# Four graph layers on one core: alternate quarters reversed in the first attention, padding columns left out in the second, an earlier operand load, a later transpose and a smaller closing product

## The chip, the cores and the metric

The kernel runs on one core of one Trainium2 chip. The metric is the device time of one execution in microseconds; the median of the runs is compared.

## The reference, cut to what matters

Four layers follow one another over 3125 nodes with 256 features and 100,000 edges, with a layer norm of the sum `x + layer(x)` behind each:

```
x = _layernorm(x + attention_4_heads(x))      # layer 0, q.k scores per edge, softmax over a node's edges
x = _layernorm(x + gat_4_heads(x))            # layer 1, leaky_relu(al_src[src] + al_dst[dst]), plus a 256-512-256 MLP
x = _layernorm(x + gin(gin(x)))               # layer 2, two plain neighbour sums with small MLPs
x = _layernorm(x + gat_1_head(gcn(x)))        # layer 3, a normalised sum, then attention with one head
...
e = jax.nn.leaky_relu(al_src[src] + al_dst[dst], NEG_SLOPE)
emax = jax.ops.segment_max(e, dst, num_segments=N)
ex = jnp.exp(e - emax[dst])
alpha = ex / denom[dst]
out = jax.ops.segment_sum(alpha[:, :, None] * h[src], dst, num_segments=N)
```

## The kernel before, in words

The graph is handled densely. Nodes are padded from N = 3125 to NPAD = 3200, 25 tiles of P = 128. Four stages run one behind the other, each a block with its own tiles and semaphores.

**Edge counts** (`build_counts`). For each tile of 128 targets the number of edges from every source is counted: VectorE writes one-hot rows (L431 to L435), TensorE multiplies them (`count`, L487) into four PSUM banks `p_g`, 400 columns each. A tile has two such counts (QPT = 2). Each ends with a closing product of zeros (L489) that adds nothing to the fourth bank and whose semaphore, `s_group`, releases ScalarE's `collect` (L552). ScalarE also writes the logarithms of the counts (L561). Between the counts TensorE does the projections of layer 0 (L174, L182) and turns count tiles for the logarithms (L497). Rows of counts, of their logarithms and of the queries, keys and values go to DRAM.

**First attention** (`attend` with `dot=True`, names `a_...`). A unit is one tile and one of 4 heads, so 100 units. A unit's 3200 weights lie in one of four buffers `sm`. TensorE's work is written out by hand in `body`, in four quarters u = 0 to 3 with TURNS = 8, 8, 8, 1 blocks of 128:

```
for u in range(ntu):
    if exists(at):
        turn(at, u)
    if dot and u in SCORE_AT and ahead(at, 2) is not None:
        score(ahead(at, 2), SCORE_AT[u])
    if behind(at, 1) is not None:
        weigh(behind(at, 1), u)
    if u == back_slot and behind(at, 2) is not None:
        turn_back(behind(at, 2))
    posts(pe, P_.pe, at, u)
```

- `turn` (L873) transposes the unit's own blocks into PSUM `p_t[u % 2]`; the trace calls its shape 128*128. It waits for the exp of its part and for the copy that frees the bank.
- `score` (L859) makes two of the eight pieces of q.k for the unit two ahead, on two halves of 64 rows at once (64*128), into `p_s[0]` and `p_s[1]`.
- `weigh` (L887) multiplies the previous unit's transposed weights by the values, 64 columns at a time (128*64). Its first quarter waits for `s_flip`, ScalarE's copy of the sums of the unit before.
- `turn_back` (L894, 128*128) turns the sums of the unit two behind. `posts` puts the output projection and norms of earlier tiles (L1267 to L1282, 128*128) into certain quarters; in this stage these are all quarters 1 and 3.

In the trace one `score` is 4 matmul records, 8 blocks of `weigh` are 16 records, and 8 of `turn` are 8. ScalarE goes through the quarters too: in each the copy of the transposed blocks back to `sm` (L930) and, in quarters 0 to 2, a part of the next unit's exp (L924); in front of them `flip` (L937), behind them `normalise` (L949). VectorE masks the two pieces of each `score` (L1010) and, during head 0 of a tile, prepares the next tile's mask from its logarithms in four parts (`mask_logs`, L997), right behind the masks of that quarter. SyncE issues the loads: `dot_tile` loads a tile's queries (L773) and its row of logarithms `full` (L777). For the first tile, the post's weights (`P_.load`) and the store of `full` come next, and only then the second tile's operands. ScalarE's queue loads the keys `kt` by head (L970) and the values (L972).

**Second attention** (`dot=False`). Two heads at a time, two passes over the 25 tiles, again 100 units. There are no scores: VectorE forms a unit's 3200 values with `lift` (L1026) and masks them and takes their maximum in `joined` (L1036); ScalarE takes the exp in three parts, EXPS = 0, 1024, 2048, 3200. TensorE's `turn`, `weigh` and `turn_back` are the same. In the second pass the posts hold the MLP with a Gelu (L1486, L1491, L1502).

**Sums and last attention** (`Tail`). Three dense neighbour sums (L1680, 25 tiles each), 25 blocks of two records a tile, with the small products of the tile before put behind certain blocks by `pe_post`. In the second sum VectorE's norm of the tile before (L1891, `x3`) is turned behind block s = 16 (L1699) and its projection follows behind s = 19. Then one attention head on full 128*128 shapes (L1757 turns, L1772 weighs).

## Time and profile before

| | us |
|---|---|
| median of 3 runs | 4048.44 |
| lowest, highest | 4046.75, 4051.8 |
| the profiled execution | 4048.74 |
| its span, first to last instruction | 4047.0 |

| engine | busy us in the span | share |
|---|---|---|
| TensorE (PE) | 3779.3 | 93% |
| TensorE weight load (PEld) | 2883.8 | 71% |
| VectorE (DVE) | 2334.7 | 58% |
| ScalarE (ACT) | 2057.9 | 51% |
| GpSimd (POOL) | 460.0 | 11% |

The span covers what lies between the first and the last instruction; 1.7 us lie around it. TensorE's busy time counts a matmul until its modelled end, so two neighbours overlap; the distance between two starts is the better measure of what an instruction costs in a stream.

### The profile page before, as it was taken

The page shows a single profiled execution, that of the slowest core. Times are in us where ns is not written, and L with a number is a line of the kernel's source. Part 1 is how long each engine was busy: PE and PEld are TensorE (multiplying, and loading weights), DVE is VectorE, ACT ScalarE, POOL GpSimd, SP SyncE. Part 2 cuts the span into 40 slices and gives each one's busy share as a digit, 9 for nine tenths or more (in the row PEclk, how much of TensorE's full clock was granted, in tenths as well). Part 3 has the DMA queues.
Part 4 walks back from the last instruction along what each step waited for, and adds up shares of the span by engine and source line. Part 5 has one row for each costly group of instructions (what it writes and reads, how often), then busy time and mean ns, then how long its engine had stood idle before and what let it go on. Part 6 is the DMA issues. An engine that isn't in the chain of part 4 may idle for free. (4 is left out here: it accounts for less than half of the span.)

```text
span 4047.0 us, 69966 instructions
## 1 busy us (share of the span) xinstructions
PE 3779.3 (93%) x27513; PEld 2883.8 (71%) x27514; DVE 2334.7 (58%) x4672; ACT 2057.9 (51%) x3697; POOL 460.0 (11%) x594
## 2 busy tenths in 40 slices
PE   4999969999999999679998988979999999999999
PEld 2656536666666666457777777768888888888888
DVE  7999935555555565289999899810012221004665
ACT  1555536666666666479998788810001000003554
POOL 0000000111111111100003455410000000000000
PEclk9999979999999999889999999989999999999999
DMA  1555572233233323153342232243333333333342
GB/s 53 234 202 234 205 239 98 90 107 107 87 105 96 103 90 108 46 200 115 115 177 100 87 108 94 92 154 141 141 141 132 132 134 136 130 130 135 137 147 69
DMA packets 177168, 521.22 MB, mean 129 GB/s; under 512 B 54304, under 2 KB 141680, under 8 KB 143728
## 3 DMA queue, kind: packets, MB, share of 16 engines
q1 hardware_dynamic: 176096, 510.62, 35.7%
q10 hardware_dynamic: 784, 6.55, 0.6%
q8 instruction: 205, 3.36, 0.3%
q14 instruction: 83, 0.68, 0.1%
HBM read 354.82 MB, written 162.29 MB: 128 GB/s over the span
## 5 line engine op out<-in xcount | busy, mean ns | idle before, releaser
L1680 PE MATMUL t_acc<-t_r,t_ct 128*128 128x256 f32 (+1 forms) x3750 | 855.7, 380 | 18.5 <-DMA t_r<-d_r 15.2
L930 ACT ACTIVATE a_sm<-a_p_t 128x1024 f32<-128x1024 f32 (+1 forms) x800 | 669.9, 837 | 340.9 <-PE a_p_t L873 333.2
L887 PE MATMUL a_p_o<-a_sm,a_v 128*64 128x128 f32 x10000 | 746.8, 281 | 69.8 <-ACT a_sumT L937 69.7
L887 PEld LDWEIGHTS a_p_o<-a_sm,a_v 128*64 128x64 f32 x10000 | 554.1, 137 | 361.2 <-issue 201.8
L1680 PEld LDWEIGHTS t_acc<-t_r,t_ct 128*128 128x128 f32 x3750 | 701.2, 190 | 112.8 <-DMA t_r<-d_r 15.6
L873 PE MATMUL a_p_t<-ident,a_sm 128*128 128x128 f32 x5000 | 714.0, 281 | 50.4 <-ACT a_sm L924 33.2
L924 ACT ACTIVATE a_sm<-a_sm,a_negm 128x1024 f32<-128x1024 f32 (+1 forms) x600 | 707.1, 1178 | 72.9 <-DVE a_negm L990 72.6
L1010 DVE CUSTOM_DVE_ANT_0 a_sm<-a_p_s,a_full 128x400 f32<-128x400 f32 x800 | 428.1, 572 | 467.0 <-PE a_p_s L859 457.9
L873 PEld LDWEIGHTS a_p_t<-ident,a_sm 128*128 128x128 f32 x5000 | 562.9, 143 | 156.5 <-issue 133.8
L859 PE MATMUL a_p_s<-a_kt,a_q 64*128 64x400 f32 x1600 | 390.4, 560 | 34.5 <-DMA a_full<-d_logs 21.2
L1026 DVE SCALAR_TENSOR_TENSOR a_sm<-a_a_bc,a_al 128x3200 f32<-128x3200 f32 x100 | 354.2, 3542 | 50.2 <-PE a_p_o L887 25.8
L1036 DVE CUSTOM_DVE_ANT_0 a_sm<-a_sm,a_mask 128x3200 f32<-128x3200 f32 x100 | 357.0, 3570 | 2.4 <-DMA a_mask<-d_full 1.7
L1772 PE MATMUL t_acc<-t_r,t_sm 128*128 128x256 f32 x1250 | 286.6, 381 | 0.0
L435 DVE TENSOR_TENSOR hot_k<-iota_w,key_g 128x2400 bf16<-128x2400 f16 x200 | 279.5, 1398 | 0.0
L552 ACT ACTIVATE ct<-p_g 128x400 f32<-128x400 f32 x200 | 149.3, 903 | 208.1 <-PE p_g L489 208.1
L1772 PEld LDWEIGHTS t_acc<-t_r,t_sm 128*128 128x128 f32 x1250 | 229.7, 190 | 31.6
L1793 ACT ACTIVATE t_hT<-t_pp 128x256 f32<-128x256 f32 x50 | 19.2, 384 | 417.9 <-PE t_pp L1699 417.9
L487 PE MATMUL p_g<-hot_k,hot_b 128*128 128x400 bf16 x1200 | 222.4, 340 | 1.8 <-DVE hot_k L435 1.8
L859 PEld LDWEIGHTS a_p_s<-a_kt,a_q 64*128 64x128 f32 x1600 | 127.0, 188 | 104.7 <-issue 70.8
L487 PEld LDWEIGHTS p_g<-hot_k,hot_b 128*128 128x128 bf16 x1200 | 116.1, 97 | 92.9 <-DVE hot_k L435 4.2
L1897 DVE TENSOR_TENSOR t_h<-t_acc,t_r 128x256 f32<-128x256 f32 x25 | 10.6, 424 | 271.7 <-PE t_acc L1680 271.7
L1822 ACT ACTIVATE t_sm<-t_p_t 128x1024 f32<-128x1024 f32 x100 | 83.6, 836 | 164.2 <-PE t_p_t L1757 164.2
(239 smaller groups left out, 3785.5 us busy)
## 6 DMA issues: line engine op xcount, KB each, us to landing
t_ct<-d_ct SPq DMA_DIRECT2D x74, 1600.0 KB, 6.7
a_mask<-d_full SPq DMA_DIRECT2D x50, 1600.0 KB, 7.0
d_logs<-logs SPq DMA_DIRECT2D x25, 1664.0 KB, 7.0
a_full<-d_logs SPq DMA_DIRECT2D x25, 1664.0 KB
d_ct<-ct SPq DMA_DIRECT2D x25, 1600.0 KB, 5.3
d_full<-a_full SPq DMA_DIRECT2D x25, 1600.0 KB, 5.6
t_ct<-d_full SPq DMA_DIRECT2D x25, 1600.0 KB, 6.9
a_a_bc<-d_as SPq DMA_DIRECT2D x8, 1600.0 KB, 10.3
```

Source lines behind the costliest of these rows:

```text
L435: v.tensor_tensor(hot_k[k][:, q, :, :, :], iota_w[:, :, :].unsqueeze(1).to_broadcast([P, TRIP // 2, GW, 2]), by_two(key_g[k][:, q, :], GW) ...
L487: last = nc.tensor.matmul(p_g[:, q, 0:GW], hot_b[k][:, q, u // 2, :, u % 2], hot_k[k][:, q, u // 2, :, u % 2], start=False, stop=u == TRIP ...
L859: nc.tensor.matmul(p_s[r][:, 0:SW], q[par][rows, h, :], kt[rows, h, k * SW:(k + 1) * SW], start=True, stop=True).then_inc(s_s, 1)
L873: m = nc.tensor.transpose(p_t[u % 2][:, i * P:(i + 1) * P], sm[buf][:, a * P:(a + 1) * P], ident[:, :])
L887: m = nc.tensor.matmul(p_o[r:r + HD, 0:P], v[:, a, (p * heads + h) * HD:(p * heads + h + 1) * HD], sm[buf][:, a * P:(a + 1) * P], start=a ...
L924: nc.scalar.activation(sm[buf][:, c], sm[buf][:, c], ACT.Exp, bias=negm[:, buf:buf + 1], accum_out=parts[:, buf, e:e + 1]).then_inc(s_prob, 1)
L930: nc.scalar.activation(sm[buf][:, a_row[u] * P:a_row[u + 1] * P], p_t[u % 2][:, 0:turns[u] * P], ACT.Copy).then_inc(s_copy, 1)
L1010: v_.tensor_tensor_reduce(out=sm[buf][:, c], in0=p_s[i % 2][:, 0:SW], in1=full[par][:, c], scale=1.0, scalar=-3.0e38, op0=ALU.add, op1=ALU ...
L1026: v_.scalar_tensor_tensor(sm[buf][:, :], a_bc[:, h, 0, :], al[gp][:, g:g + 1], a_bc[:, h, 1, :], ALU.add, ALU.max).then_inc(s_lift, 1)
L1036: v_.tensor_tensor_reduce(out=sm[buf][:, :], in0=sm[buf][:, :], in1=mask[gp][:, :], scale=1.0, scalar=-3.0e38, op0=ALU.add, op1=ALU.max, a ...
L1680: m = self.nc.tensor.matmul(self.acc[t % 2][:, 0:width], self.ct[t % 3][:, a * P:(a + 1) * P], rows[:, a, 0:width], start=a == 0, stop=a = ...
L1772: m = self.nc.tensor.matmul(self.acc[t % 2][:, 0:D], self.sm[j % 2][:, a * P:(a + 1) * P], self.r[1][:, a, :], start=a == 0, stop=a == NT - 1)
```

## The change

1. The closing product of a count is 16 columns wide (GD) in place of 400 (GW).
2. In the first attention, quarters 1 and 3 run `weigh`, `score`, `turn` in place of `turn`, `score`, `weigh`. Quarters 0 and 2, and the whole second attention, keep their order.
3. In the second attention `lift`, `joined` and the last exp leave out the 75 padding columns. VectorE clears the values' last block and the buffers' padding once; the values are loaded in two pieces behind that, the second with the last block's 53 real rows.
4. In the first attention the second tile's queries and logarithms are issued right behind the first tile's.
5. In the second neighbour sum the turned `x3` moves from block 16 to 17, its projection from 19 to 20.

```diff
@@ count @@
-                    nc.tensor.matmul(p_g[:, QUAD - 1, 0:GW], zeros[0:1, 0:P], zeros[0:1, :], start=False, stop=True, skip_group_check=True).then_inc(s_group, 1)
+                    nc.tensor.matmul(p_g[:, QUAD - 1, 0:GD], zeros[0:1, 0:P], zeros[0:1, 0:GD], start=False, stop=True, skip_group_check=True).then_inc(s_group, 1)
@@ attend @@
+        exps = EXPS if dot else EXPS[:-1] + [N]
+        s_pad = sem("padding_cleared")
@@ sync @@
-                def dot_tile(j, par, half, first=False, last=False):
-                    if not first:
-                        wait_alone(sp, s_mask, (j - 1) * heads)
+                def dot_load(j, par, half):
+                    if j >= 2:
+                        sp.wait_ge(s_mask, (j - 1) * heads)
...
+                def dot_tile(j, par, half, first=False, last=False):
+                    if j != 1:
+                        dot_load(j, par, half)
                     if first:
+                        dot_load(1, 1, 0)
                         sp.wait_ge(s_in[0], 16 * n_in)
                         P_.load(sp)
@@ gat_tile @@
-                        sp.dma_start(v[:, :, :], v_dram).then_inc(s_v, 16)
+                        sp.wait_ge(s_pad, 1)
+                        sp.dma_start(v[:, 0:NT - 1, :], v_dram[:, 0:NT - 1, :]).then_inc(s_v, 16)
+                        sp.dma_start(v[0:N - (NT - 1) * P, NT - 1, :], v_dram[0:N - (NT - 1) * P, NT - 1, :]).then_inc(s_v, 16)
@@ tensor: weigh, body @@
-                        pe.wait_ge(s_v, 16)
+                        pe.wait_ge(s_v, 16 if dot else 32)
...
-                        if exists(at):
+                        turns_first = not dot or u % 2 == 0
+                        if turns_first and exists(at):
                             turn(at, u)
+                        if not turns_first and behind(at, 1) is not None:
+                            weigh(behind(at, 1), u)
                         if dot and u in SCORE_AT and ahead(at, 2) is not None:
                             score(ahead(at, 2), SCORE_AT[u])
-                        if behind(at, 1) is not None:
+                        if turns_first and behind(at, 1) is not None:
                             weigh(behind(at, 1), u)
+                        if not turns_first and exists(at):
+                            turn(at, u)
@@ scalar, vector @@
-                    c = slice(EXPS[e], EXPS[e + 1])
+                    c = slice(exps[e], exps[e + 1])
...
-                    v_.scalar_tensor_tensor(sm[buf][:, :], a_bc[:, h, 0, :], al[gp][:, g:g + 1], a_bc[:, h, 1, :], ALU.add, ALU.max).then_inc(s_lift, 1)
+                    v_.scalar_tensor_tensor(sm[buf][:, 0:N], a_bc[:, h, 0, 0:N], al[gp][:, g:g + 1], a_bc[:, h, 1, 0:N], ALU.add, ALU.max).then_inc(s_lift, 1)
...
-                    v_.tensor_tensor_reduce(out=sm[buf][:, :], in0=sm[buf][:, :], in1=mask[gp][:, :], scale=1.0, scalar=-3.0e38,
+                    v_.tensor_tensor_reduce(out=sm[buf][:, 0:N], in0=sm[buf][:, 0:N], in1=mask[gp][:, 0:N], scale=1.0, scalar=-3.0e38,
...
+                if not dot:
+                    v_.memset(v[:, NT - 1, :], 0.0).then_inc(s_pad, 1)
+                    for b in range(4):
+                        v_.memset(sm[b][:, N:NPAD], 0.0)
@@ Tail.pe_post @@
-        if k == 1 and s == 16:
+        if k == 1 and s == 17:
...
-        if k == 1 and s == 19:
+        if k == 1 and s == 20:
```

TensorE in the middle of the first attention, before: one unit from its first scores to `turn_back`. `x8` are blocks; L873 is `turn`, L859 `score`, L887 `weigh`, L894 `turn_back`.

```order
L859 MATMUL a_p_s<-a_kt,a_q 128x400 x2
L887 MATMUL a_p_o<-a_sm,a_v 64x128 x8
L873 MATMUL a_p_t<-ident,a_sm 128x128 x8
L859 MATMUL a_p_s<-a_kt,a_q 128x400 x2
L887 MATMUL a_p_o<-a_sm,a_v 64x128 x8
L873 MATMUL a_p_t<-ident,a_sm 128x128 x8
L859 MATMUL a_p_s<-a_kt,a_q 128x400 x2
L887 MATMUL a_p_o<-a_sm,a_v 64x128 x8
L873 MATMUL a_p_t<-ident,a_sm 128x128
L859 MATMUL a_p_s<-a_kt,a_q 128x400 x2
L887 MATMUL a_p_o<-a_sm,a_v 64x128
L894 MATMUL a_p_t<-a_twice,a_sumT 128x64
```

The same place in the changed kernel, one unit from its first `turn` (L882 is now `turn`, L868 `score`, L896 `weigh`, L903 `turn_back`):

```order
L882 MATMUL a_p_t<-ident,a_sm 128x128 x8
L868 MATMUL a_p_s<-a_kt,a_q 128x400 x2
L896 MATMUL a_p_o<-a_sm,a_v 64x128 x16
L868 MATMUL a_p_s<-a_kt,a_q 128x400 x2
L882 MATMUL a_p_t<-ident,a_sm 128x128 x16
L868 MATMUL a_p_s<-a_kt,a_q 128x400 x2
L896 MATMUL a_p_o<-a_sm,a_v 64x128 x9
L868 MATMUL a_p_s<-a_kt,a_q 128x400 x2
L882 MATMUL a_p_t<-ident,a_sm 128x128
L903 MATMUL a_p_t<-a_twice,a_sumT 128x64
L882 MATMUL a_p_t<-ident,a_sm 128x128 x8
```

The `weigh` of quarters 0 and 1 are now neighbours (x16), so are those of quarters 2 and 3 (x9) and the `turn` of quarters 1 and 2 (x16), and the single `turn` of quarter 3 stands beside `turn_back` and the next unit's first `turn`.

SyncE's queue at the start of the first attention, before:

```order
L773 DMA a_q<-d_q 64x2x128 x4
L777 DMA a_full<-d_logs 128x3328
L1169 DMA a_wout<-in_Wout 128x2x256
L1169 DMA a_w<-in_L_W 128x2x256
L1171 DMA a_bout<-in_bout 128x256
L1171 DMA a_ln_g<-in_L_ln_g 128x256
L1171 DMA a_ln_b<-in_L_ln_b 128x256
L1171 DMA a_gat_b<-in_L_gat_b 128x256
L785 DMA d_full<-a_full 128x3200
L773 DMA a_q<-d_q 64x2x128 x4
L777 DMA a_full<-d_logs 128x3328
```

and in the changed kernel (L775 loads queries, L779 logarithms, L792 stores `full`):

```order
L775 DMA a_q<-d_q 64x2x128 x4
L779 DMA a_full<-d_logs 128x3328
L775 DMA a_q<-d_q 64x2x128 x4
L779 DMA a_full<-d_logs 128x3328
L1187 DMA a_wout<-in_Wout 128x2x256
L1187 DMA a_w<-in_L_W 128x2x256
L1189 DMA a_bout<-in_bout 128x256
L1189 DMA a_ln_g<-in_L_ln_g 128x256
L1189 DMA a_ln_b<-in_L_ln_b 128x256
L1189 DMA a_gat_b<-in_L_gat_b 128x256
L792 DMA d_full<-a_full 128x3200
```

The second tile's five loads moved ahead of the six loads of the post's weights and the store of the first `full`.

## Rows read from the trace of the kernel before

**Rows 1.** Busy time by stretch: length, PE, PEld, DVE, ACT, POOL, clock, DMA share, GB/s.
```profile
530.00:1700.00 1170.00, 1124.17 (x9600) 746.70 (x9600) 632.88 (x2204) 749.14 (x1351) 129.72 (x227) 0.97 0.32 102
```

**Rows 2.** Timeline of TensorE, one unit of the first attention (start, length, engine, line).
```profile
1197.59 1.04 PE L873 MATMUL a_p_t<-ident,a_sm 128*128 128x128 f32 x8
1198.56 0.94 PE L859 MATMUL a_p_s<-a_kt,a_q 64*128 64x400 f32 x4
1199.43 1.09 PE L887 MATMUL a_p_o<-a_sm,a_v 128*64 128x128 f32 x16
1200.46 1.09 PE L873 MATMUL a_p_t<-ident,a_sm 128*128 128x128 f32 x8
1201.48 0.94 PE L859 MATMUL a_p_s<-a_kt,a_q 64*128 64x400 f32 x4
...
1206.30 0.33 PE L873 MATMUL a_p_t<-ident,a_sm 128*128 128x128 f32 x1
1206.56 0.94 PE L859 MATMUL a_p_s<-a_kt,a_q 64*128 64x400 f32 x4
1207.43 0.43 PE L887 MATMUL a_p_o<-a_sm,a_v 128*64 128x128 f32 x2
1207.79 0.43 PE L894 MATMUL a_p_t<-a_twice,a_sumT 128*128 128x64 f32 x2
1208.07 0.39 PE L873 MATMUL a_p_t<-ident,a_sm 128*128 128x128 f32 x2
```

**Rows 3.** Timeline of TensorE in the last attention.
```profile
3750.56 1.04 PE L1757 MATMUL t_p_t<-ident,t_sm 128*128 128x128 f32 x8
3751.43 0.60 PE L1772 MATMUL t_acc<-t_r,t_sm 128*128 128x256 f32 x2
3751.87 1.04 PE L1757 MATMUL t_p_t<-ident,t_sm 128*128 128x128 f32 x8
```

**Rows 4.** Timeline of ScalarE, the same unit.
```profile
1198.06 0.27 ACT L937 ACTIVATE a_sumT<-a_p_o 128x128 f32<-128x128 f32 x1
1198.67 1.02 ACT L930 ACTIVATE a_sm<-a_p_t 128x1024 f32<-128x1024 f32 x1 [0.34 <-PE a_p_t L873]
1199.59 1.14 ACT L924 ACTIVATE a_sm<-a_sm,a_negm 128x1024 f32<-128x1024 f32 x1
...
1205.43 1.25 ACT L924 ACTIVATE a_sm<-a_sm,a_negm 128x1152 f32<-128x1152 f32 x1
```

**Rows 5.** Timeline of VectorE, the same unit.
```profile
1202.46 0.57 DVE L1010 CUSTOM_DVE_ANT_0 a_sm<-a_p_s,a_full 128x400 f32<-128x400 f32 x1 [0.24 <-PE a_p_s L859]
...
1203.45 1.02 DVE L997 SCALAR_TENSOR_TENSOR a_full<-a_full 128x832 f32<-128x832 f32 x1
```

**Rows 6.** Timeline of the first attention's start.
```profile
560.79 0.93 PEld L859 LDWEIGHTS a_p_s<-a_kt,a_q 64*128 64x128 f32 x4 [1.45 <-DMA a_kt<-d_kt]
...
584.92 1.03 DVE L997 SCALAR_TENSOR_TENSOR a_full<-a_full 128x832 f32<-128x832 f32 x1 [10.18 <-DMA a_full<-d_logs]
...
586.50 2.19 PE L859 MATMUL a_p_s<-a_kt,a_q 64*128 64x400 f32 x4 [9.36 <-DVE a_mx L1010]
```

**Rows 7.** Timeline of TensorE in the edge counts.
```profile
307.50 0.34 PE L489 MATMUL p_g<-zeros 1*128 1x400 bf16 x1
307.77 2.05 PE L174 MATMUL p_qk<-xT,w_qk 128*128 128x128 f32 x16
```

**Rows 8.** Waits in the edge counts, from 75 to 515 (us, times, longest).
```profile
PE p_g L487 <- DVE hot_k L435: 0.4, 1, 0.4
```

**Rows 9.** Groups by line, the second attention's two wide operations.
```profile
L1036 DVE CUSTOM_DVE_ANT_0 a_sm<-a_sm,a_mask 128x3200 f32<-128x3200 f32 x100 | 357.0, 3570 | 2.4 <-DMA a_mask<-d_full 1.7 <-issue 0.6
L1026 DVE SCALAR_TENSOR_TENSOR a_sm<-a_a_bc,a_al 128x3200 f32<-128x3200 f32 x100 | 354.2, 3542 | 50.2 <-PE a_p_o L887 25.8 <-DMA a_a_bc<-d_as 17.5 <-DMA a_al<-d_ad 6.8
```

**Rows 10.** Timeline of TensorE in the second attention's second pass.
```profile
2463.39 0.88 PE L887 MATMUL a_p_o<-a_sm,a_v 128*64 128x128 f32 x12 [2.45 <-ACT a_sumT L937]
```

**Rows 11.** Who waited for the tile that L1891 writes (line, us, times).
```profile
  PEld t_pp L1699: 10.0, 25
```

## The prediction, made before the changed kernel was run

> **What bounds the kernel now.** I read busy time by stretch first, then TensorE's timeline inside each stretch, then the waits. In the first attention TensorE is busy 1124 of 1170 us [rows 1], and inside a unit no row of TensorE has a wait: each run of one kind starts as soon as the one before is issued [rows 2]. A unit lasts 1208.07 - 1197.59 = 10.48 us. So this stage is bound by what TensorE's instructions cost to issue, and the distance between starts shows that cost. Eight `turn` blocks take 1201.48 - 1200.46 = 1.02, one takes 1206.56 - 1206.30 = 0.26. That is (1.02 - 0.26) / 7 = 0.109 a block and 0.15 that each run pays once. Eight `weigh` blocks take 1.03: the same 0.15 over 8 x 0.109. The first `turn` of a unit, which follows `turn_back` of the same shape 128*128, takes 0.97, which is 0.05 less. So I split the 0.15 into 0.05 on entering a shape and 0.10 on leaving it. A `score` takes 0.87 or 0.88 in every place, whatever stands around it. In the last attention, where `turn` and `weigh` have the same shape, eight `turn` take 3751.43 - 3750.56 = 0.87 = 8 x 0.109, with nothing for the change of work [rows 3]. The price hangs on the shape, not on the kind of work or its semaphores.
>
> **Edge counts.** TensorE waited for VectorE's one-hot rows once, 0.4 us [rows 8]; it sets the pace. From the closing product to the next start are 307.77 - 307.50 = 0.27 us, and ScalarE's `collect` waits for its end, 0.34 [rows 7]. The 384 columns left out are 384 / 2.4 GHz = 0.16 us at the full clock, off both the issue and the end. There are 50 such products (2 x 25): **-8 us**. Bounds: nothing, if VectorE turns out to be as slow as TensorE, and 50 x 0.27 = 13.5. I take 8, since both paths out of the product become shorter by the same amount. The Trainium skill, TensorEngine Tiling, section Instruction Overhead, says that a matmul with one column has the latency of one with 60. By it only 340 columns would be gained, and the term would be 7 in place of 8.
>
> **First attention, the order.** Before, each quarter pays `turn` to `score` 0.10, `score` to `weigh` 0.05, and `weigh` to a 128*128 shape 0.10 + 0.05: 0.30, so 1.20 a unit. Now half a unit pays `turn` to `score` 0.10, `score` to `weigh` 0.05, `weigh` to `score` and `score` to `turn`; `weigh` to `weigh` and `turn` to `turn` are free. The last two changes of shape stand nowhere in the trace. Built from the parts they cost 0.10 (leaving `weigh`) and 0.05 (entering `turn`), since `score` itself showed no surcharge. Then a unit pays 0.60 and saves 0.60. Bounds: if each new change cost 0.15, the saving is 0.30; if both were free, 0.90. I take 0.60: the 0.97 against 1.02 supports the split. The posts stand in quarters 1 and 3, behind 128*128 work after the change as before it, and bring no extra change of shape. With 98 full units: **-59 us** (29 to 88).
>
> Does another engine now become late? Starts in the new unit of 9.87 us, from the same prices: `turn` 0, `score` 0.97, `weigh` 1.84 and 2.77, `score` 3.74, `turn` 4.61 and 5.54, `score` 6.51, `weigh` 7.38 and 8.30, `score` 8.61, single `turn` 9.48, `turn_back` 9.65. ScalarE copies 1198.67 - 1197.59 = 1.08 us after the first `turn` starts [rows 2, 4], 0.05 later where the shape is entered anew. It takes 0.92 from a copy to the next work, 1.14 for an exp of 1024 columns, 1.25 for the longer one. So: copy 1.08, exp 2.00, idle from 3.14, copy 5.74, exp 6.66, copy 7.80, exp 8.72, last copy 9.97, `normalise` and `flip` (0.27) until about 10.7. The next unit's `weigh` needs that `flip` at 9.87 + 1.84 = 11.71: one us to spare. The post that copies the projections out once a tile takes half of it at most. VectorE starts its masks 0.98 after a `score` starts and has done both 0.99 later [rows 2, 5], after which the bank is free; with the reading of the maxima some 2.05 after the start. The closest two scores are now 2.10 apart (before, 0.87 + 1.02 + 0.26 = 2.15). In head 0, 0.99 + 1.02 of `mask_logs` fit too [rows 5], with almost nothing over. I count no stall, but this is the tightest place: 0.1 us more a unit would be 10.
>
> **First attention, the start.** VectorE waits 10.18 us for the second tile's logarithms, with the masks that TensorE needs queued behind; TensorE stands 9.36 us [rows 6]. These loads wait in the queue behind the post's weights and the first store. Issued behind the first tile's, they are ahead of all that. What is late next are the keys of the second head: they were already waited for [rows 6], and the 1.7 MB in front of them can cost up to 3 us. Afterwards TensorE ran at 1.2 GHz, half its clock: four records of `score` take 2.19 against 0.94 [rows 2, 6]. With the stop gone, the scores and blocks behind it should run at the full clock, worth 2 or 3 us. Between 3 and 13, I take **-9 us**.
>
> **Second attention.** VectorE spends 3.57 and 3.54 us a unit on two operations of 3200 columns; its idle time in front of them is 2.4 and 50.2 us in all, of which 25.8 is waiting for TensorE and the rest the start's loads [rows 9]. The waits for TensorE all lie in the second pass, so in the first pass VectorE sets the pace. 75 of 3200 columns less are 0.08 each, 0.16 a unit, times 50 units: 8. In the second pass TensorE stands for ScalarE, 2.45 us a tile behind exp, Gelu and `flip` [rows 10]. There VectorE has slack, and only the shorter exp counts. (1.25 - 1.14) / 128 columns x 75 is 0.06 [rows 4], times 25: 1.5. Bounds of the second pass: 0 and 8. The extra values' load holds up the second tile's operands by half a us. The five clears fall into the wait for the first load. **-9 us**.
>
> **Second sum.** The load of the turned `x3` waited for VectorE 25 times, 10.0 us in all, 0.40 each [rows 11]. One block later is 0.44 us (3751.87 - 3751.43, the same shape) [rows 3], so the wait goes. As a weight load runs ahead of its product, about half of it reached TensorE's path: **-5 us** (0 to 10). The projection, one block later too, still has four blocks, 4 x 0.44 us, behind it for VectorE's one operation on 256 columns.
>
> **Sum.** 8 + 59 + 9 + 9 + 5 = 90. From the profiled execution's 4048.7 (span 4047.0 and 1.7 around it) that gives 3959; the median of the runs, 4048.4, is the same within 0.3. A measurement of this kernel tells 0.2%, 8 us, from no change.
>
> **Rivals.** (A) *The price hangs on something else that the order keeps.* Then the order saves nothing and the time is 3959 + 59 = 4018. The last attention's 0.87 speaks against it [rows 3]. 5%. (B) *The new changes of shape cost the full 0.15 each.* That adds 2 x (0.05 + 0.10) = 0.30 a unit, 29 us: 3988. For it speaks that neither pair was ever seen; against it that `score` added nothing to its neighbours. 10%. The Trainium skill, TensorEngine Tiling, section Key Properties, says "Changing tiling mode (not just tile) drains the TensorE"; with one drain for every change it would give this rival's time. The trace agrees that a change of shape costs and a change of work does not, but shows no equal price. (C) *VectorE paces the first attention.* The closest scores leave 0.05 us. If every unit loses 0.15 the time is 3974. 10%. (D) *ScalarE's `flip` comes late and it is slower.* The odd quarters leave ScalarE idle from 3.14 to 5.74 and push its work to the end of the unit. The kernel gets slower from the point where the first `weigh` stands 0.9 us a unit, that is `flip` 1.9 later than worked out. At 2.1 later, 1.1 x 98 = 108 us are lost: 4067. Nothing in rows 4 makes its sequence that long. 2%. The forecast itself has 73%.
>
> **How the numbers follow.** The likeliest time is 3959. The range reaches down to 3943 (the second pass gains as much as the first, the start 12, `score` hides part of a change) and up to 3989, which takes in B and C. Only A and D would not be clearly inside or faster; A is faster too. Faster 0.97, same 0.01, slower 0.02.
>
> **What the profile of the changed kernel would show.** A unit of the first attention of 9.9 us without a wait on TensorE; `weigh` x32 or x18 in one run; `score` behind `weigh` 0.10 after its last step. No wait of 10 us near 585. Closing products with 0.11 to the next start. Wide operations of 3.46 and 3.49 us, and a first pass 0.16 us a unit shorter. No wait of L1699. A stall of TensorE on L1010 (C) or on the copy of the sums (D) would prove the placing wrong; a unit of 10.2 us without stalls would be B.

## The result, and the profile after

The median is 4028.7 us (10 runs, 4011.5 to 4042.6) against 4051.2 for the kernel before, measured in between (10 runs, 4046.8 to 4062.5). The ratio is 0.9938, 95% interval 0.9925 to 0.9951: 0.6% faster, where 2.2% were forecast. That is small but clear of no change. The profiled execution took 4030.3, its span is 4028.5. Its runs lie 31 us apart, those of the kernel before 16.

Both traces cut at the same places (the first `score`, the issue of the second attention's first mask load, the first block of the first sum, the first `turn` of the last attention) show where the time went:

| stage, us | before | after | change | forecast |
|---|---|---|---|---|
| edge counts, to the first `score` | 549.2 | 541.9 | -7.3 | -8 |
| first attention | 1162.9 | 1126.2 | -36.7 | -68 |
| second attention | 977.0 | 1005.0 | **+28.0** | -9 |
| three sums | 1005.8 | 1002.1 | -3.7 | -5 |
| last attention | 352.0 | 353.3 | +1.3 | 0 |

**Edge counts.** TensorE's timeline after, the closing product and what follows it:
```profile
303.63 0.18 PE L489 MATMUL p_g<-zeros 1*128 1x16 bf16 x1
303.74 2.05 PE L174 MATMUL p_qk<-xT,w_qk 128*128 128x128 f32 x16
```
The distance to the next start fell from 0.27 [rows 7] to 0.11, by the 0.16 that was worked out.

**First attention.** TensorE's timeline after, one unit (it answers to rows 2):
```profile
900.87 0.94 PE L868 MATMUL a_p_s<-a_kt,a_q 64*128 64x400 f32 x4
901.74 1.97 PE L896 MATMUL a_p_o<-a_sm,a_v 128*64 128x128 f32 x32
903.64 0.94 PE L868 MATMUL a_p_s<-a_kt,a_q 64*128 64x400 f32 x4
904.51 1.97 PE L882 MATMUL a_p_t<-ident,a_sm 128*128 128x128 f32 x16
906.41 0.94 PE L868 MATMUL a_p_s<-a_kt,a_q 64*128 64x400 f32 x4
907.28 1.30 PE L896 MATMUL a_p_o<-a_sm,a_v 128*64 128x128 f32 x18
908.52 0.94 PE L868 MATMUL a_p_s<-a_kt,a_q 64*128 64x400 f32 x4
909.39 0.33 PE L882 MATMUL a_p_t<-ident,a_sm 128*128 128x128 f32 x1
909.56 0.33 PE L903 MATMUL a_p_t<-a_twice,a_sumT 128*128 128x64 f32 x2
909.73 1.04 PE L882 MATMUL a_p_t<-ident,a_sm 128*128 128x128 f32 x8
910.70 0.94 PE L868 MATMUL a_p_s<-a_kt,a_q 64*128 64x400 f32 x4
```
From `score` to `score` are 910.70 - 900.87 = 9.83 us, 0.65 less than before. 16 blocks of `weigh` take 1.90, which is 16 x 0.109 and one 0.15, and `score` to `turn` is 0.87. The prices of the forecast hold. But a tile should be 4 such units and its posts, 41.5 us (44.19 before), and from the second tile on it takes from 41.5 to 46.9. TensorE's and ScalarE's timelines at the post where 23 tiles lose about 1 us each:
```profile
930.16 0.33 PE L882 MATMUL a_p_t<-ident,a_sm 128*128 128x128 f32 x1
930.32 0.33 PE L903 MATMUL a_p_t<-a_twice,a_sumT 128*128 128x64 f32 x2
931.78 0.41 PE L1285 MATMUL a_pp<-ident,a_o_t 128*128 128x128 f32 x2 [1.12 <-ACT a_as L1317]
```
```profile
929.83 1.25 ACT L938 ACTIVATE a_sm<-a_sm,a_negm 128x1152 f32<-128x1152 f32 x1
930.97 0.20 ACT L938 ACTIVATION_READ_ACCUMULATOR a_sm<-a_sm,a_negm 128x1 f32 x1
931.06 0.38 ACT L1314 ACTIVATE a_v<-a_pp 128x256 f32<-128x256 f32 x1
931.33 0.18 ACT L1315 ACTIVATE a_ad<-a_pp 128x4 f32<-128x4 f32 x1
931.38 0.19 ACT L1316 ACTIVATE a_as<-a_pp 128x4 f32<-128x4 f32 x1
931.44 0.20 ACT L1317 ACTIVATE a_as<-a_pp 128x4 f32<-128x4 f32 x1
```
The post L1285 in head 2, quarter 3 writes `pp`, and ScalarE must first have copied an older tile's projections out of it (L1314 to L1317). In the new order ScalarE's third exp starts late in the unit, and these copies end 1.0 us after TensorE is at the post. Two waits of the stage after, from 640 to 1660 (us in all, times, longest), are new or have grown; below them is the second as it was before, from 640 to 1700:
```profile
DVE a_sm L1024 <- remote: 22.8, 10, 4.0
PE a_pp L1285 <- ACT a_as L1317: 22.7, 23, 2.2
```
```profile
PE a_pp L1267 <- ACT a_as L1299: 1.7, 2, 0.9
```
The first is VectorE, which starts masks late; "remote" says that no engine's work was found to have released it. These ten waits are not all of it. Set against the start of its own `score`, one of the two masks of the second `score` in head 2 is over 0.3 us late in 15 tiles after, by up to 2.9 us, and in 6 tiles before, by up to 1.45 (of the tiles from the third on).

**Second attention.** VectorE's groups of the two wide operations, which answer to rows 9:
```profile
L1050 DVE CUSTOM_DVE_ANT_0 a_sm<-a_sm,a_mask 128x3125 f32<-128x3125 f32 x100 | 349.8, 3498 | 1.1 <-DMA a_mask<-d_full 1.1
L1040 DVE SCALAR_TENSOR_TENSOR a_sm<-a_a_bc,a_al 128x3125 f32<-128x3125 f32 x100 | 346.6, 3466 | 89.2 <-PE a_p_o L896 63.0 <-DMA a_a_bc<-d_as 17.9 <-DMA a_al<-d_ad 8.3
```
They are shorter by 0.07 and 0.08 as forecast, and 24 tiles of the first pass went from 352.6 to 347.4. But VectorE now waits 63.0 us for TensorE, against 25.8. Busy time by stretch in the second pass (the columns of rows 1), before and after, and within one tile after:
```profile
2180.00:2660.00 480.00, 427.47 (x3971) 343.38 (x3971) 417.63 (x591) 380.70 (x664) 231.38 (x200) 0.95 0.27 92
```
```profile
2180.00:2660.00 480.00, 427.69 (x3570) 340.23 (x3568) 373.26 (x547) 338.83 (x599) 208.20 (x196) 0.86 0.25 83
...
2446.00:2452.50 6.50, 4.47 (x44) 3.59 (x42) 6.36 (x10) 5.01 (x13) 6.17 (x5) 0.97 0.34 95
2452.50:2459.30 6.80, 6.44 (x27) 4.59 (x27) 6.63 (x11) 3.74 (x6) 1.83 (x2) 0.53 0.62 232
2459.30:2469.90 10.60, 10.60 (x116) 8.95 (x116) 6.84 (x9) 9.11 (x16) 2.62 (x4) 1.00 0.01 2
```
TensorE did 10% less in the same 480 us at a granted clock of 0.86 in place of 0.95. The pass has 22 such stops, and at each from the fourth on the clock falls to half (0.53 is 1.2 GHz with an edge of the stretch at 2.4) for 6.8 us. TensorE's timeline there:
```profile
2449.42 1.04 PE L882 MATMUL a_p_t<-ident,a_sm 128*128 128x128 f32 x8
2452.86 1.97 PE L896 MATMUL a_p_o<-a_sm,a_v 128*64 128x128 f32 x16 [2.39 <-ACT a_sumT L951]
2454.76 3.78 PE L1509 MATMUL a_pp<-a_w,a_zT 128*128 128x256 f32 x8
```
The stop is the one of rows 10, 2.39 where it was 2.45, but behind it 8 blocks of `weigh` (16 records) take 1.97 us in place of 1.09. Most tiles took 21.1 us before, about every third 22.7 with a half-clock stretch of 3.4 us, and two in a row 23.9. Now 18 in a row, from the fourth stop to the last, take 23.9.

**Sums.** No wait for `x3` is left. The waits of TensorE's weight loads from 2690 on (us, times, longest; the rest are 0.7 or less):
```profile
PEld t_p_t L1775 <- ACT t_sm L1835: 4.8, 1, 4.8
PEld t_acc L1698 <- DMA t_ct<-d_ct: 4.2, 1, 4.2
PEld t_pp L1717 <- DVE t_y L1921: 1.8, 1, 1.8
```

### The profile page after: what moved, and what is told of

The parts are those of the page before. It is cut to its first block and busy times, and to the rows that moved or that the text cites. A ratio compares the mean times of both kernels' runs of the same rounds, so it can differ in the third digit from the quotient of the medians.

```text
span 4028.5 us, 69973 instructions
## 1 busy us (share of the span) xinstructions
PE 3751.9 (93%) x27513; PEld 2918.0 (72%) x27514; DVE 2316.3 (57%) x4677; ACT 2036.2 (51%) x3697; POOL 474.7 (12%) x594
## 5 line engine op out<-in xcount | busy, mean ns | idle before, releaser
L896 PE MATMUL a_p_o<-a_sm,a_v 128*64 128x128 f32 x10000 | 720.0, 284 | 61.1 <-ACT a_sumT L951 58.4
L882 PE MATMUL a_p_t<-ident,a_sm 128*128 128x128 f32 x5000 | 702.0, 280 | 51.4 <-ACT a_sm L938 33.8
L896 PEld LDWEIGHTS a_p_o<-a_sm,a_v 128*64 128x64 f32 x10000 | 572.0, 140 | 241.6 <-issue 117.5
L938 ACT ACTIVATE a_sm<-a_sm,a_negm 128x1024 f32<-128x1024 f32 (+2 forms) x600 | 701.1, 1168 | 67.1 <-DVE a_negm L1004 66.8
L882 PEld LDWEIGHTS a_p_t<-ident,a_sm 128*128 128x128 f32 x5000 | 564.0, 143 | 223.1 <-issue 196.4
L868 PE MATMUL a_p_s<-a_kt,a_q 64*128 64x400 f32 x1600 | 396.1, 558 | 29.8 <-DMA a_full<-d_logs 21.7
L1040 DVE SCALAR_TENSOR_TENSOR a_sm<-a_a_bc,a_al 128x3125 f32<-128x3125 f32 x100 | 346.6, 3466 | 89.2 <-PE a_p_o L896 63.0
L1050 DVE CUSTOM_DVE_ANT_0 a_sm<-a_sm,a_mask 128x3125 f32<-128x3125 f32 x100 | 349.8, 3498 | 1.1 <-DMA a_mask<-d_full 1.1
L868 PEld LDWEIGHTS a_p_s<-a_kt,a_q 64*128 64x128 f32 x1600 | 130.2, 187 | 110.2 <-issue 64.5
```

Of the source, the lines that this page charges most:

```text
L868: nc.tensor.matmul(p_s[r][:, 0:SW], q[par][rows, h, :], kt[rows, h, k * SW:(k + 1) * SW], start=True, stop=True).then_inc(s_s, 1)
L882: m = nc.tensor.transpose(p_t[u % 2][:, i * P:(i + 1) * P], sm[buf][:, a * P:(a + 1) * P], ident[:, :])
L896: m = nc.tensor.matmul(p_o[r:r + HD, 0:P], v[:, a, (p * heads + h) * HD:(p * heads + h + 1) * HD], sm[buf][:, a * P:(a + 1) * P], start=a ...
L938: nc.scalar.activation(sm[buf][:, c], sm[buf][:, c], ACT.Exp, bias=negm[:, buf:buf + 1], accum_out=parts[:, buf, e:e + 1]).then_inc(s_prob, 1)
L1040: v_.scalar_tensor_tensor(sm[buf][:, 0:N], a_bc[:, h, 0, 0:N], al[gp][:, g:g + 1], a_bc[:, h, 1, 0:N], ALU.add, ALU.max).then_inc(s_lift, 1)
L1050: v_.tensor_tensor_reduce(out=sm[buf][:, 0:N], in0=sm[buf][:, 0:N], in1=mask[gp][:, 0:N], scale=1.0, scalar=-3.0e38, op0=ALU.add, op1=ALU. ...
```

## The experiments

Every experiment kernel has bounds checks on loop numbers that VectorE and TensorE load once a tile in the edge counts: on all of them in the first four, on two in the others. after_b and after_c are the changed kernel with just these: 4074.1 and 4033.9. The checks lengthen the edge counts (to 590.0 and 545.7 us, from 541.9), so the stages behind them are compared directly. All of them, from the profiled executions (us; "96 units" runs from `turn_back` 1 to 97 of the first attention, "pass 2" over 25 tiles of the second):

| kernel | median | first att. | 96 units | second att. | pass 2 |
|---|---|---|---|---|---|
| before | 4051.2 | 1162.9 | 1054.9 | 977.0 | 531.8 |
| after | 4028.7 | 1126.2 | 1031.0 | 1005.0 | 563.8 |
| after_b | 4074.1 | 1124.0 | 1025.2 | 1009.8 | 569.2 |
| no_pad | 4047.5 | 1121.1 | 1026.1 | 977.6 | 530.6 |
| only_order | 4061.5 | 1136.3 | 1031.1 | 976.4 | 530.7 |
| only_pad | 4113.5 | 1162.6 | 1055.8 | 1003.6 | 564.1 |
| after_c | 4033.9 | 1129.2 | 1032.1 | 1011.9 | 571.4 |
| pad_first | 4009.9 | 1132.8 | 1035.8 | 973.4 | 532.6 |
| no_gelu | 3979.4 | 1142.9 | 1045.5 | 942.3 | 504.0 |
| values_early | 4009.2 | 1105.9 | 1010.3 | 989.5 | 546.8 |
| small_load | 4025.3 | 1134.6 | 1038.4 | 1005.2 | 566.3 |
| load_later | 4002.1 | 1107.5 | 1010.0 | 981.3 | 539.8 |
| both_fixes | 3980.9 | 1101.2 | 1006.2 | 972.2 | 532.6 |
| three_fixes | **3964.2** | 1091.7 | 996.7 | 975.0 | 535.6 |
| exp_short | 4035.0 | 1135.6 | 1036.0 | 998.5 | 556.8 |
| lift_short | 4006.6 | 1131.1 | 1035.7 | 970.2 | 530.0 |
| exp_h0 | 4010.8 | 1139.6 | 1041.2 | 972.2 | 532.8 |
| exp_h1 | 4028.9 | 1138.3 | 1039.1 | 1011.9 | 570.5 |

Each stage time is that of one execution. Where its code is the changed kernel's, the first attention varies from 1121 to 1143 between them, and its first 96 units from 1025 to 1046. The profiled executions of after_c (4044.4) and exp_h1 (4051.1) are among the slower ones of their kernels.

**Which part brings what.** The first four are the changed kernel, the changed kernel without the padding part of the diff, and the kernel before with one part alone.

after_b: 

> The changed kernel as it is, with runtime bounds checks on the loop numbers that VectorE and TensorE load once a tile in the edge counts (every experiment kernel has them, so this one is their measure). Both theories: 4029 to 4040, as the checks can cost at most a few tenths of a us in each of 25 tiles; first attention some 1126 long, second 1005.

no_pad: 

> The changed kernel with the padding columns put back into the second attention. Theory 1 (leaving the padding out moved the timing of the second pass so that TensorE's stop behind exp, Gelu and flip brings half clock in every tile): the second pass goes back to tiles of 21.1 and 22.7 us, the second attention to 977, the time to 28 below the changed kernel, about 4001. Theory 2 (what the stages before do decides it, not the padding): tiles stay at 23.9, and the first pass loses 8: about 4037.

only_order: 

> The kernel before with the order of the first attention alone. Theory 3 (ScalarE's copies of the projections end behind turn_back, and TensorE's post in head 2, quarter 3 stands behind them, about 1 us a tile): a tile of the first attention of about 43 us, 30 us saved: 4018. Theory 4 (the irregular delays come from the moved load and its place in the queue): tiles of 42.5 or less, 45 us saved or more: 4003. By theory 1 the second attention stays at 977; by theory 2 it becomes 1010 and the time 4050.

only_pad: 

> The kernel before with the padding columns left out of the second attention, nothing else. Theory 1: second attention 1005 in place of 977, time about 4077. Theory 2: first pass 8 shorter, second pass as before or 1.5 shorter, time about 4039.

after_b came out at 4074, 34 above the expected end: the checks cost 45 us, and that was badly judged. The times expected of the other three are short by 36 to 47 as well, so the stages are what tells. Both kernels that leave the padding out have a second attention of 1004 to 1010, both that keep it 976 to 978, whatever stands ahead: theory 1's part on the padding holds and theory 2 falls. The order alone gives the same first attention as the whole change but for its start (96 units 1031.1), so theory 4 falls: the moved load is not behind the irregular delays. The start: from the first `score` to the first `turn_back` the trace shows 60.5 us in only_order and 50.8 in no_pad, which has the early load too. That is 9.6 for the load (forecast 9). But the kernels with the early load lie between 50.1 and 53.9 there, so it is known to be 7 to 10 and no better.

only_pad has the old order, and one of the two masks of that second `score` is late in 12 of its tiles, by up to 2.5 us. All but two of its full tiles still take 44.19, the same as before. So VectorE starts late in the old order too, less often and by less, and the old order has room for it where the new one has none.

**The second pass.** pad_first and no_gelu:
```diff
-                    v_.scalar_tensor_tensor(sm[buf][:, 0:N], a_bc[:, h, 0, 0:N], ...
+                    v_.scalar_tensor_tensor(sm[buf][:, 0:(N if p == 0 else NPAD)], a_bc[:, h, 0, 0:(N if p == 0 else NPAD)], ...
```
```diff
-                        a = nc.scalar.activation(zT[:, f, :], pz[:, f * P:(f + 1) * P], ACT.Gelu, bias=b1[:, f:f + 1])
+                        a = nc.scalar.activation(zT[:, f, :], pz[:, f * P:(f + 1) * P], ACT.Identity, bias=b1[:, f:f + 1])
```
In pad_first `joined` and the exp have the same condition.

pad_first: 

> The changed kernel with the padding left out in the first pass of the second attention only; the second pass works on all 3200 columns again. Theory 1 (the second pass falls into a rhythm with half clock in every tile when its tiles are a little shorter): first pass 8 shorter, second pass as before the change, second attention 969 in place of 1005. Rival (the clock follows what the first pass did): tiles stay at 23.9, second attention 1005 or more.

no_gelu: 

> The changed kernel with Identity in place of Gelu, so that ScalarE changes no function table in the second pass; the output leaves out the Gelu. Theory 1 (the low clock comes behind the stop of TensorE for exp, Gelu and flip): the stop of 2.4 us and the wait behind the second table load go, the clock stays full, tiles of 17.5 to 19 in place of 23.9, second attention under 890. Rival (half clock without the stop): tiles over 21, stretches of half clock remain.

pad_first has 973.4: the first pass keeps its gain and the second is as before. no_gelu leaves out the Gelu. Without it there is no stretch at half clock; the busy time of 2250 to 2600:
```profile
2250.00:2600.00 350.00, 316.43 (x3052) 254.95 (x3051) 314.28 (x457) 244.93 (x476) 216.40 (x155) 1.00 0.29 97
```
So the low clock comes behind the stop that Gelu and its table loads make. But a tile takes 20.9 us, not 17.5 to 19, and the second attention 942.3, not under 890: from 2300 to 2500 VectorE is busy 94%, which leaves a tile little to gain. The stop itself is worth 0.1 us (20.9 against the 21.0 of a tile after at full clock); what it does to the clock is worth 3 us a tile.

Next, which of the shortened operations it takes. In exp_short only the exp is shorter in the second pass, in lift_short only `lift`, in exp_h0 and exp_h1 the exp of one head:
```diff
-                    c = slice(exps[e], exps[e + 1])
+                    c = slice(EXPS[e], EXPS[e + 1] if e < NE - 1 else (NPAD if dot or (at[0] == 1 and at[4] == 0) else N))
```
This is exp_h1; `== 1` at the end is exp_h0. ScalarE takes the exp of head 1 directly ahead of Gelu.

exp_short: 

> The changed kernel with VectorE on 3200 columns again in the second pass of the second attention, and only ScalarE's exp 75 columns shorter there (the other columns are left as VectorE wrote them, which the sums leave out). Theory 1 in its narrower form (VectorE's two wide operations hold the tile at 21.1, and their 0.16 us a unit are what lets it fall into the rhythm): second attention 973, tiles of 21.1 and 22.7. Rival (the shorter exp is enough, as it comes ahead of the stop): tiles of 23.9, 1005.

after_c: 

> The changed kernel as it is, with bounds checks on two of the loop numbers a tile only, as the later experiment kernels have them. It gives their common measure: 3 to 5 us of checks above the changed kernel's 4029, so 4033.

lift_short: 

> The changed kernel; in the second pass of the second attention only VectorE's first wide operation (lift) leaves out the padding, while its second and ScalarE's exp work on 3200 columns. Theory 7 (only the exp ahead of TensorE's stop decides the rhythm, VectorE's length does not): tiles of 21.1 and 22.7, second attention 973. Rival 7b (any shortening makes the tile fall into it): tiles of 23.9, 1005.

exp_h0: 

> The changed kernel; in the second pass VectorE works on 3200 columns, and the exp is 75 columns shorter for head 0 alone, which does not stand directly ahead of the Gelu. Theory 7 in its narrow form (the exp that stands ahead of Gelu and flip): tiles of 21.1 and 22.7, 973. Rival 7c (either head's exp will do): 23.9 in most tiles, 998 or more.

exp_h1: 

> As the kernel before it, with the exp shorter for head 1 alone, the one that ScalarE does directly ahead of the Gelu. Theory 7: 23.9 in most tiles, 998 or more. If it is the sum over a tile that counts: the same as for head 0.

exp_short went against the theory: 998.5 and tiles of 23.9 from the seventh stop on, with VectorE's full 3200 columns. VectorE's length is not what counts; lift_short has 970.2, the shortest second attention of all that keep Gelu. (A shorter `joined` alone was not run.) And of the two heads, one. The product that ends a post (L1510, two records a tile) in exp_h0, and then in exp_h1, both from 2380 to 2500:
```profile
L1510 PE MATMUL a_pp<-a_b,a_ones x10: 374/426/498, 2393.4 to 2479.8; 1*128 1x256 f32 x10
```
```profile
L1510 PE MATMUL a_pp<-a_b,a_ones x10: 375/523/671, 2386.7 to 2482.8; 1*128 1x256 f32 x10
```
The busy time from 2250 to 2600, again exp_h0 first:
```profile
2250.00:2600.00 350.00, 310.77 (x2885) 249.99 (x2886) 316.43 (x439) 285.03 (x495) 170.97 (x149) 0.95 0.29 97
```
```profile
2250.00:2600.00 350.00, 314.14 (x2666) 250.73 (x2665) 295.79 (x400) 264.01 (x457) 160.55 (x133) 0.86 0.28 93
```
Four tiles take 86 us in the one and 96 in the other, at 0.95 and 0.86 of the clock. In these two executions the exp directly ahead of the stop, 0.06 us shorter, costs 38 us over the pass (570.5 against 532.8).

38 us is the most that it costs, though, and not what it costs each time. The profiled exp_h1 is the slowest of its 8 runs; the medians of the two kernels are 18 us apart (4028.9 against 4010.8, of 8 and 2 runs). What the step decides is seen by putting all traces together. In the eight kernels with Gelu and the full exp ahead of the stop, a tile with a stretch of 6.8 us takes 24.0, 23.95 and 23.92 us, three times at most in a row, and then the clock falls less again. In the nine with the shorter exp, a tile of 23.9 is followed by tiles of 23.9 to the end of the pass. They differ in when that begins: at the first stop in exp_h1 and after_c, at the fourth in after, at the twelfth in values_early and the fifteenth in load_later. The runs fit this. Those of exp_h1 go from 4000.6 us at a granted clock of 0.972 to 4051.1 at 0.958, those of after_c from 4003.4 at 0.972 to 4053.1 at 0.959; the kernels with the full exp and four or more runs lie within 20 us each. So theory 7 holds for what keeps the pass in long tiles; what brings the first one about was not looked for.

Why such a little step can do it: with the shorter exp a long tile takes 23.90 us, and the stretches of half clock also start 23.90 apart (2404.3, 2428.2, 2452.1 in the trace after). The tile then meets the fall of the clock in the same phase each time, and nothing leads out; below, the pass is called locked. That both numbers are the same is shown; that this is what holds it is a reading of it.

**The first attention.** values_early, small_load and load_later:
```diff
-                if (lag, s) == (2, 10):
+                if (lag, s) == (2, 9):
                     act.wait_ge(PE_.sem, PE_.at(jj, "proj"))
```
```diff
-                    sp.dma_start(full[par][:, :], row(log_dram, j)).then_inc(s_in[par], 16)
+                    rows = slice(0, P if isinstance(j, int) and j < 2 else 8)
+                    sp.dma_start(full[par][rows, :], row(log_dram, j)[rows, :]).then_inc(s_in[par], 16)
```
```diff
-                        sp.wait_ge(s_mask, (j - 1) * heads)
+                        sp.wait_ge(s_mask, (j - 1) * heads + 1)
```
From the third tile on, small_load leaves out 120 of the 128 rows of logarithms and their scaling.

values_early: 

> The changed kernel with ScalarE's four copies of the projections one quarter earlier, so that they are done when TensorE comes to the post behind turn_back in head 2. Theory 3 (that post waits for these copies, 1.05 us in each of 24 tiles): the wait goes, first attention 1100 in place of 1124, if the later flip does not take its place. Rival 3b (flip is then what is late, as ScalarE's work in that unit is the same): 1115 or more, with the wait on the next weigh.

small_load: 

> The changed kernel with 8 of 128 rows of logarithms loaded for tiles 2 to 24 of the first attention, so 1.5 MB less DMA a tile; masks of later tiles are then wrong. Theory 5 (VectorE's late masks come from its code being loaded while the tile's logarithms fill the same DMA engines): its waits of 23 us on other things than TensorE fall under 8, and the scattered delays of TensorE, some 16 us, under 6; first attention 1110. Rival 5b (the late masks have to do with the order of VectorE's own work): both stay, 1124.

load_later: 

> The changed kernel with SyncE's loads of a tile's queries and logarithms (tiles 2 to 24) one unit later. In the first attention VectorE starts a pair of masks 1 to 4 us late in about 10 of 24 tiles, always at the same place: the second score of head 2, 3 us after these loads are issued. Theory 6 (VectorE is held up while these loads go out): the late pairs move to a place one unit later, 3 to 5 us behind the loads. Rival 6b (that place in VectorE's own code is slow): they stay behind the reciprocal of head 2. If the new place has slack, first attention 1110, otherwise 1126 either way.

TensorE's wait in values_early, from 640 to 1660:
```profile
PE a_pp L1285 <- ACT a_as L1317: 0.8, 1, 0.8
```
It fell from 22.7 us (25.0 in after_c) to 0.8, and 96 units took 1010.3, 22 us less than in after_c. That is theory 3; `flip` did not take its place (two waits, 1.2 us in all). Its second pass is locked only in its last ten tiles, which is the rest of its gain and luck of phase.

small_load left the delays as they were (VectorE's waits of the kind were 35.5 us): the bytes of the load are not the cause, theory 5 falls. The place is nearly always the same, the second `score` of head 2; in a few tiles the third is late too. VectorE, SyncE and TensorE in the trace after:
```profile
879.92 0.17 DVE L1070 RECIPROCAL a_rden<-a_den 128x1 f32<-128x1 f32 x1
883.92 0.58 DVE L1024 CUSTOM_DVE_ANT_0 a_sm<-a_p_s,a_full 128x400 f32<-128x400 f32 x1 [3.84 <-remote]
```
```profile
877.50 2.48 SPq L775 DMA_DIRECT2D a_q<-d_q  x4
880.02 0.59 SPq L779 DMA_DIRECT2D a_full<-d_logs  x1
880.66 0.43 SPq L768 DMA_DIRECT2D d_full<-a_full  x1
```
```profile
880.39 0.94 PE L868 MATMUL a_p_s<-a_kt,a_q 64*128 64x400 f32 x4
...
884.55 1.43 PE L868 MATMUL a_p_s<-a_kt,a_q 64*128 64x400 f32 x4 [0.43 <-DVE a_mx L1024]
```
The masks of the `score` at 880.39 start at 883.92, 2.6 us later than usual, and the next `score` waits for the bank. SyncE has just issued the next but one tile's loads. With these one unit later VectorE's waits of that kind, from 640 to 1640, are:
```profile
DVE a_sm L1024 <- remote: 4.4, 2, 2.8
```
The masks of that `score` are then late in 5 tiles in place of 15, and 96 units take 1010.0 in place of 1032.1. About 9 us of these 22 are not VectorE's: the wait at L1285 was 15.8 here and 25.0 in after_c. So the loads' issue has to do with the late masks (theory 6), but they did not move with them as expected: they went. Those that are left stand at the old place, behind L1070.

The trace also has the packets that bring the engines' code, in two queues of their own. In 9 of the 15 late tiles after, none of them runs between 3 us before the mask is due and its start, and late code does not explain these. In all nine the load of `full` was issued 1.3 to 1.8 us before the mask was due, but so it was in tiles that were on time. In the other 6, and in all 5 of load_later, such a packet does run then; whether it holds VectorE up was not tested. What passes between the loads' issue and that place in VectorE's code stays open. The second attention of load_later, 981.3, owes its gain to a pass that is locked in its last seven tiles only, which is luck again.

**All together.** both_fixes is values_early and pad_first; three_fixes has load_later too.

both_fixes: 

> The changed kernel with ScalarE's copies of the projections a quarter earlier and the padding left out in the first pass of the second attention only. If the two effects add: first attention 1106, second 973, 3993 in all, against 4010 and 4009 for each alone. If the second pass can fall into the rhythm of half clock with full columns too: over 4010.

three_fixes: 

> As the kernel with both changes, and the loads of the first attention one unit later. By theory 6 with slack at the new place 3980; by rival 6b 3993.

They beat both kernels, and what was expected of them (3993, and 3980 or 3993): 3980.9, ratio to the kernel before 0.9822 (0.9807 to 0.9837), and 3964.2, ratio 0.9779 (0.9763 to 0.9795), the latter with 10 us between its runs in place of 31. They have the two shortest first attentions of all, and their second passes, with the full exp, are not locked. In three_fixes 16 of 24 tiles of the first attention take 41.51 or 41.52 us, and 96 units take 996.7. Beside values_early, moving the loads is worth 10 us of these units (1006.2 to 996.7) and 17 of the median.

## Why the prediction was right or wrong

The profiled execution should have been 90 us shorter and was 18. The miss is 37 in the second attention, 31 in the first, 3 elsewhere. Two steps failed: the price of the second pass, and the placing of the other engines' work in the first attention.

- **Edge counts, -8:** right, 7.3. The bound "if VectorE turns out to be as slow as TensorE" is what the kernels with all checks show: with the change or without, their edge counts end at 589.7 to 590.2.
- **The order, -59:** the price of the changes of shape was right, 0.65 a unit where 0.60 was worked out. 96 units of it are 1054.9 - 62.4 = 992.5; three_fixes has 996.7. The measured 4029 lies near rival A's 4018, and A is wrong all the same: the units without a wait are 0.65 shorter. The Trainium skill, TensorEngine Tiling, section Key Properties, says that a change of tiling mode drains TensorE, and gives no price. The trace agrees that a change costs something, and shows that the price is not the same everywhere: a run of `weigh` or `turn` pays 0.15 in all, a `score` takes 0.87 with either behind it.
- **"Does another engine now become late?":** the step that failed in the first attention. It placed ScalarE's work against `flip` alone. The sentence "The post that copies the projections out once a tile takes half of it at most" is true of `flip`, and overlooks who else waits for that post: TensorE's own L1285, in the same bank, 2.1 us before `flip` is due. That is 22.7 us of waiting in the trace after, and 22 of 96 units in values_early. A wait in the queue had to be looked up for the posts too, not only for the unit's own steps. Rival D had the late ScalarE, with the wrong waiter and price.
- **VectorE, "the tightest place":** the masks of undisturbed pairs start 0.97 after the `score` as before, so rival C as put is wrong. But in 15 tiles a mask came late by up to 2.9 us, in the trace before in 6 by up to 1.45. The forecast took each mask's start from one unit that had none late. There was room for them before (only_pad) and there is none now. 96 units after are 38.5 above the 992.5; 22.7 of it is the post, which leaves some 16 us for VectorE, an estimate. Moving the loads gave 10 (three_fixes against both_fixes) to 13 (load_later, its 22 less 9 of the post's).
- **The start, -9:** right, 7 to 10.
- **Second attention, first pass, -8:** 5 to 7 in 24 tiles.
- **Second pass, -1.5, bounds 0 and 8:** the step that failed in the second attention, and the larger miss: it took 32 us more (563.8 against 531.8), so it was wrong by 33 and outside its bounds. The text had the stop of 2.45 us, read only its length off, and let "only the shorter exp counts" stand for a gain. The runs show that this very exp, shorter, lets the pass stay in tiles of 23.9 us with 6.8 us at half clock in each. The trace before had tiles of 21.1, every third or so of 22.7, and two of 23.9: in some the clock fell behind the stop and in others not. That was not read, and the bound at zero had no reason. How much is lost is in part chance, since the long tiles begin earlier or later from run to run.
- **Second sum, -5:** 3.7, and 1.3 lost again at the start of the last attention, where the first blocks of `turn` and `weigh` behind the unchanged stop of 4.4 us ran longer at half clock (16 records in 4.71 us, before 3.62).
- **The range, 3943 to 3989,** held neither miss. The rival that was missing is a stop once a tile which the change leaves in place, and behind which it alters the clock.

## What to carry to other kernels

When one engine's work is moved, list for every instruction behind it on that engine who waits for it, the posts of other tiles too, and set its end against that waiter's start. Where TensorE stops once a tile, as here for 2.4 us, look at the granted clock of several tiles. If some tiles have a half-clock stretch and others not, a small step directly ahead of the stop can decide it: here 0.06 us did, and it cost up to 3 us a tile. Change it alone, look at tile lengths, and take several runs, since one profile can be the best or the worst of them. A part of a change that gains in one loop can be kept there and left out in the next.

## What the runs showed of the hardware that was not expected

- TensorE's clock and a loop can lock: with the tile 23.90 us long and the falls of the clock 23.90 us apart, up to 21 tiles in a row had 6.8 us at 1.2 GHz (18 in after, 21 in exp_h1). 75 columns of one exp, 0.06 us, decide whether it holds. The Trainium skill, TensorE: Matmul & The Clock Gate, section What's actually happening, tells of a gate with two rates; the trace agrees (stretches at half and full clock only).
- VectorE can start an operation up to 2.9 us later than usual behind its `score` (4.6 in exp_h0), at one place of its code, while no engine's work and no load is found that it waited for. It nearly goes away when SyncE's loads are issued at another time (5 tiles in place of 15). The Trainium skill, Perfetto Trace Analysis, section DMA Instruction — HWDGE (DVE, Sync), says that VectorE's and SyncE's sequencers share the block that makes descriptors; VectorE issues no transfer here, and at 883.92 it starts 2.8 us after the end of SyncE's last issue, so no run shows that this is it.
- Bounds checks on 12 loop numbers of VectorE and 4 of TensorE a tile cost 45 us over 25 tiles (after_b against after, by the medians); on two each, the edge counts end 2 to 4 us later (543.9 to 545.8 against 541.9).
